# Turning the first quad's maxima into PSUM bank 5 instead of bank 7

## The chip, the cores and the metric

The kernel runs on one core of a Trainium2 chip. A time is the device time of one launch in microseconds (us). A comparison is made between medians of several launches on the same chip.

## What is computed

Two layers of a small transformer, on x of shape 2 x 512 x 128 and a context of 2 x 154 x 128, all in float32 with reference accuracy:

```python
x = x + L0_xattn(layernorm(x), ctx, ctx, Wq, bq, Wk, bk, Wv, bv, Wo, bo)   # 16 heads of 8
x = x + L0_ffn(layernorm(x), ...)      # 8 experts, each takes its top 128 tokens
x = x + L1_xattn(layernorm(x), ctx, mask, W_attn)                          # one head, masked
x = x + L1_ffn(layernorm(x), ...)      # 32 experts of width 64, top 8 per token, and a shared one
```

The change lies in the first of the four, the attention of 16 heads:

```python
scores = einsum('bhqd,bhkd->bhqk', q, k) / sqrt(HEAD_DIM)
attn = softmax(scores, axis=-1)
out = einsum('bhqk,bhkd->bhqd', attn, v) @ Wo.T + bo
```

## The kernel before

The kernel is one program per engine, written out by hand. TensorE (`pe`), VectorE (`dve`), ScalarE (`act`), GpSimd (`pool`) and SyncE (`sp`, DMA issues) each run their list of steps in the order in which it is written, and every dependence is a wait on a semaphore that another engine counts up. An engine that waits holds up all that stands behind the wait in its list.

PSUM is one tensor `bank` of 8 banks with 512 float32 columns each. The first attention works in quads: 4 heads of one batch of 512 queries, 8 quads in all, called `cc` 0 to 7. For a quad, the steps are:

- `keys(g)` multiplies the keys of head group g (4 groups, both batches) into `keys_bank(g)`: bank 3, 4, 7 and 7. ScalarE copies them with their bias to `kh`, rounded to a shorter format; VectorE's `k_lo(g)` (L540) reads the bank again and writes the rounding error beside it, partitions 64 to 95. The semaphore `klo_ready` counts these. `expand` (GpSimd L388, for quad 0 VectorE L598) spreads the keys of a group over a block per head in `ks`.
- `turned`, `first_queries` and `all_queries` make the queries. For quads 1 to 7 three DMA copies each (`laid`, L337, L338, L340) bring them to their partitions in `qs`; semaphores `laid0` and `laid1`.
- `rough(cc, part)` (L1383) makes trial products of queries and keys. VectorE's `maxima(cc, part)` (L572) reduces them to the largest value for each query and head, into `smax`; semaphore `max_done`. For quad 0 there are two parts, which lie in banks 0 to 2 and 3 to 5; for the others six, in banks 0 to 2.
- TensorE's `maxima(cc)` turns `smax` by four transposes (helper `turn`, L1302) into bank 7, and ScalarE's `minus_max(cc)` (L1008) copies the result, negated, into `qs` as extra rows, so that `scores` (L1428) gives scores minus the maximum. Semaphores `mT_psum` and `mT_ready`.
- `scores`, ScalarE's `exponents` (L1054) and `attend` (L1442, into bank 5, first at `attend(0, 0)`) are the softmax and the products with the values; `values` (L1376) makes the values in bank 6.

Two helpers on TensorE guard the banks that many steps share. `take7` waits for the reader of whoever used bank 7 before, and notes who will be the next reader:

```python
free7 = [(Z["klo_ready"], 4)]

def take7(sem_, count):
    pe.wait_ge(*free7[0])
    free7[0] = (sem_, count)
```

The first user of bank 7 after the last group's keys is `maxima(0)`, so that it waits for `klo_ready` at 4, that is `k_lo(3)`. Bank 5 is first used for the gate sums (L1516); ScalarE reads them out (L1046, semaphore `gsum_ready`), and the second part of quad 0's trial products, which reaches into bank 5, waits for that.

Around the change the orders are, on TensorE: `rough(0, 0)`, `all_queries(0)`, `keys(3)`, `rough(0, 1)`, four filling products (`early_work`, L1328, bank 0), `maxima(0)`, `values(0, 0)`, `scores(0, 0)`, `rough(1, 0)`. On VectorE:

```python
maxima(0, 0)
all_q_lo(0)
maxima(0, 1)
k_lo(3)
dve.wait_ge(L["x1"], 16)
second = measure(x, TB)
maxima(1, 0)
```

`measure` takes the statistics of the second half of x (L504 to L514); GpSimd raises the variance to the power -0.5 (L368) and VectorE centres that half (L526) after `maxima(1, 3)`. On SyncE the load of `fc1` (2048 KB, L344) stands between the copies for quad 3 and those for quad 4.

Of the kernel before, what the change touches and what calls it, by code (L numbers as in the profile page):

```python
# [13 lines left out]
P = 128  # L14
# [3 lines left out]
TB = T // B  # L18
# [10 lines left out]
HQ = HH // 2  # L29
QW = HQ * DH  # L30
KQ = 3 * QW + HQ
QUADS = 2 * COMBOS
QSLOTS = 6
# [51 lines left out]
def maxes(cc, part):  # L85

    return part + 1 if cc == 0 else 2 + PARTS * (cc - 1) + part + 1
# [13 lines left out]
def build(nc, x_d, ctx2_d, mask_d, watt_d, pack_d, rows_d, gate_d, fc1_d, fc2_d, wout_d, wr_d, rec_d,  # L101
          bd_d, out_d):
    with ExitStack() as ctx:
        def sb(name, shape, dt=F32):
            return ctx.enter_context(nc.sbuf_tensor(name, shape, dt))

        def sem(name):
            return ctx.enter_context(nc.semaphore(name))

        def lay(base, names, parts=P):  # L110

            out, at = [], 0
            for shape in names:
                n = int(np.prod(shape[1:]))
                v = base[0:shape[0], at:at + n]
                ax = "abcd"[:len(shape) - 1]
                if len(shape) > 2:
                    v = v.rearrange(f"p ({' '.join(ax)}) -> p {' '.join(ax)}",
                                    **{a: m for a, m in zip(ax, shape[1:])})
                out.append(v)  # L120
                at += n
            assert at <= base.shape[1], (at, base.shape)
            return out

        bank = ctx.enter_context(nc.psum_tensor("bank", [P, 8, 512], F32))
# [29 lines left out]
        qs, ks = lay(arena_a, ([P, QSLOTS, S], [P, QUADS, HBLK * P]))  # L155
# [46 lines left out]
        smax = sb("smax", [P, 2 * TB, QW + HQ])  # L202
# [67 lines left out]
        Z = {n: sem(n) for n in names}  # L270
# [695 lines left out]
        def _(act):  # L966
# [37 lines left out]
            def minus_max(cc):  # L1004

                r0, turns = (0, cc) if cc < 2 else (cc % 2 * QW, 1 + cc // 2)
                act.wait_ge(Z["mT_psum"], turns + 1)
                act.mul(qs[3 * QW:KQ, cc % QSLOTS, :], bank[r0:r0 + HQ, 7, :], -1.0).then_inc(Z["mT_ready"], 1)  # L1008

            def with_bias(b, c0=0, c1=S):  # L1010
                act.wait_ge(Z["at_psum"], b + 1 + (c0 > 0))
# [47 lines left out]
            act.wait_ge(L["late"], 48)  # L1059
            indicators(act.copy, 0)  # L1060
            minus_max(0)
            exponents(0, 0)
            exponents(0, 1)
# [4 lines left out]
            turned(1)  # L1068
            exponents(0, 4)
            minus_max(1)  # L1070
            all_queries(1)
            exponents(0, 5)
            exponents(0, 6)
            exponents(0, 7)
            exponents(0, 8)
            exponents(0, 9)
            minus_max(2)
            minus_max(3)
            exponents(1, 0)
# [220 lines left out]
        def _(pe):  # L1300
            def turn(dst, src, n=P):
                return pe.transpose(dst, src, ident[0:n, 0:n])  # L1302
# [17 lines left out]
# [4 lines that stand above are left out]
# [83 lines left out]

            def maxima(cc, both=False):

                take7(Z["mT_ready"], cc + 1 + both)  # L1410
                pe.wait_ge(Z["max_done"], maxes(cc + both, PARTS - 1 if cc else 1))
                q0, q1 = (0, QW + HQ) if both else (cc % 2 * QW, cc % 2 * QW + HQ)
                for i in range(TB):
                    ins = turn(bank[0:q1 - q0, 7, i * P:(i + 1) * P], smax[:, cc // 2 % 2 * TB + i, q0:q1])
                ins.then_inc(Z["mT_psum"], 1)

            def scores(c, i):
# [105 lines left out]
            pe.wait_ge(Z["max_done"], 1)  # L1523
            early_work(4, 0)
            maxima(0)
            values(0, 0)
            scores(0, 0)
# [12 lines left out]
            turned(1)  # L1540
            rough(2, 1)
            maxima(1)
            all_queries(1)
            rough(2, 2)
# [16 lines left out]
            attend(0, 1)  # L1561
            rough(4, 1)
            maxima(2, both=True)
            rough(4, 2)
            rough(4, 3)
# [89 lines left out]
            for b in range(B):  # L1655
                pe.matmul(bank[0:SH, 0, b * D:(b + 1) * D], ctx2[:, b, 0:SH], wout[:, 0, :], start=True, stop=True)
                ins = pe.matmul(bank[0:SH, 0, (B + b) * D:(B + b + 1) * D], ctx2[:, b, SH:SK], wout[:, 0, :],
                                start=True, stop=True)
# [49 lines left out]
            for t in range(T):  # L1708
                ins = pe.matmul(upto, onesb[:, :], gteq[:, 0, t, None, :].broadcast_to([P, T, E0]),
                                start=False, stop=(t == T - 1))  # L1710
# [422 lines left out]
```

## Time and profile before

| | us |
|---|---|
| median of 3 runs | 244.21 (244.19 to 244.49) |
| the profiled execution | 244.43 |
| its span | 242.6 |

| engine | busy us | share of the span |
|---|---|---|
| TensorE, products | 224.3 | 92% |
| TensorE, weight loads | 157.4 | 65% |
| VectorE | 175.9 | 72% |
| ScalarE | 128.8 | 53% |
| GpSimd | 74.6 | 31% |

The profile is of one execution. Times within it are counted from the start of its span. In the rows PE is TensorE and PEld its weight loads, DVE is VectorE, ACT is ScalarE, POOL is GpSimd, SPq is SyncE's DMA queue. A float32 product appears as two MATMUL instructions. L1302 is the line of the helper `turn`, so all transposes carry it; their operands tell them apart, and `smax` means the turns of maxima. An idle time in brackets is that of the engine before the first instruction of the row, with what ended it. The chain is followed back from the last instruction; "issue" in it is time in which an engine waited for nothing visible.

### The profile page before, as it was taken

What the parts mean: (1) busy time and instruction counts of PE and PEld (TensorE: products, weight loads), DVE (VectorE), ACT (ScalarE), POOL (GpSimd) and SP (SyncE); (2) the same over time, 40 slices, a digit from 0 to 9 for tenths busy, and PEclk for the clock granted to TensorE, in tenths of its full rate; (3) what the DMA queues carried; (4) which work ended last, traced back from release to release, by engine and by line L of the source; (5) the groups of instructions that cost most, each with busy time, mean ns of one, the idle gap of its engine ahead of it and who ended that gap; (6) DMA issues with size and microseconds to landing.
All of it is one profiled execution on the core that took longest, in us unless ns stands there. A gap on an engine that the chain in (4) does not pass through costs nothing.

```text
span 242.6 us, 3703 instructions
## 1 busy us (share of the span) xinstructions
PE 224.3 (92%) x1220; PEld 157.4 (65%) x1228; DVE 175.9 (72%) x436; ACT 128.8 (53%) x262; POOL 74.6 (31%) x113
## 2 busy tenths in 40 slices
PE   8979998999997888999999998889999999999993
PEld 2446544655564344678687966667888888888871
DVE  2689766663376887796351787999888879888883
ACT  2427557678536921442544766666454555554551
POOL 6235997020430600000490303000453353353000
PEclk9999999999999999999999999979999999999999
DMA  6316739300000000000052000000112212200002
GB/s 226 123 43 195 263 87 352 118 0 0 3 0 0 1 0 4 0 0 3 1 139 80 0 3 1 0 0 0 46 43 49 81 47 48 83 0 0 3 0 86
DMA packets 6152, 12.92 MB, mean 53 GB/s; under 512 B 1139, under 2 KB 2259, under 8 KB 5878
## 3 DMA queue, kind: packets, MB, share of 16 engines
q1 hardware_dynamic: 5302, 11.91, 15.8%
q10 hardware_dynamic: 832, 0.78, 1.0%
q8 instruction: 10, 0.16, 0.3%
q14 instruction: 8, 0.07, 0.1%
HBM read 10.78 MB, written 0.52 MB: 47 GB/s over the span
## 4 chain that ended last, share of the span: by engine, by line
PE 74%; DVE 18%; ACT 3%; issue 3%; POOL 1%; DVEq 0%; another core or an unknown queue 0%; ACTq 0%; POOLq 0%
PE bank L1939 6%; PE bank L1943 6%; PE bank L1940 6%; PE bank L1302 5%; PE bank L1442 5%; PE bank L1428 5%; DVE att L707 4%; PE bank L1383 4%; PE bank L1973 3%; PE bank L1789 3%; PE bank L1976 3%; PE bank L1328 3%; PE bank L1974 3%; PE bank L1954 3%; PE bank L1776 3%
## 5 line engine op out<-in xcount | busy, mean ns | idle before, releaser
L1242 ACT ACTIVATE arena_d<-bank,bias 128x512 f32<-128x512 f32 x34 | 23.4, 689 | 32.3 <-PE bank L1943 32.3
L893 DVE SCALAR_TENSOR_TENSOR arena_d<-bank,bias,arena_d 128x512 f32<-128x512 f32 x34 | 25.5, 750 | 9.5 <-ACT arena_d L1242 9.2
L572 DVE TENSOR_REDUCE smax<-bank 128x3 f32<-128x462 f32 (+2 forms) x44 | 25.2, 619 | 8.4 <-PE bank L1383 8.3
L1054 ACT ACTIVATE arena_c<-bank 128x512 f32<-128x512 f32 x40 | 22.6, 598 | 10.2 <-PE bank L1442 5.4
L471 POOL CAST arena_b<-rec 128x512 fp32r<-128x512 f32 x17 | 13.4, 788 | 46.7 <-PE bank L1976 46.6
L1939 PE MATMUL bank<-arena_b 128*128 128x512 f32 x68 | 27.1, 399 | 0.1
L1943 PE MATMUL bank<-arena_b 128*128 128x512 f32 x68 | 27.1, 398 | 0.0
L1940 PE MATMUL bank<-arena_b 128*128 128x512 f32 x68 | 27.0, 397 | 0.0
L907 DVE TENSOR_TENSOR arena_a<-arena_d,arena_a 128x512 fp32r<-128x512 f32 x34 | 23.5, 691 | 0.8 <-ACT arena_a L1249 0.7
L1249 ACT CAST arena_a<-arena_d 128x512 fp32r<-128x512 f32 x34 | 20.8, 612 | 3.2 <-DVE arena_d L902 2.9
L902 DVE TENSOR_TENSOR arena_d<-arena_d,bank 128x512 f32<-128x512 f32 x32 | 21.8, 681 | 0.4 <-PE bank L1954 0.3
L368 POOL TENSOR_TENSOR rstd<-vareps,neghalf 128x4 f32<-128x4 f32 x8 | 8.1, 1012 | 38.5 <-DVE vareps L514 28.5
L1383 PE MATMUL bank<-arena_a 96*128 96x462 f32 (+3 forms) x64 | 17.6, 353 | 0.6 <-DVE smax L572 0.4
L1308 PE MATMUL bank<-pack,onesb 128*128 128x512 bf16 x66 | 17.3, 378 | 0.3
L1428 PE MATMUL bank<-arena_a 100*128 100x512 f32 x40 | 17.3, 454 | 0.0
L474 POOL TENSOR_TENSOR arena_b<-rec,arena_b 128x384 fp32r<-128x384 f32 x17 | 16.3, 961 | 1.4
L1383 PEld LDWEIGHTS bank<-arena_a 96*128 96x128 f32 x64 | 11.3, 189 | 7.6 <-DVE smax L572 3.1
L1943 PEld LDWEIGHTS bank<-arena_b 128*128 128x128 f32 x68 | 13.1, 192 | 3.2 <-DVE arena_b L858 0.4
L1939 PEld LDWEIGHTS bank<-arena_b 128*128 128x128 f32 x68 | 12.9, 190 | 3.2 <-issue 0.3
L1940 PEld LDWEIGHTS bank<-arena_b 128*128 128x128 f32 x68 | 13.0, 191 | 2.7
L1973 PE MATMUL bank<-arena_a,arena_b 128*128 128x512 f32 x34 | 13.9, 408 | 0.3 <-ACT arena_a L1249 0.3
L1976 PE MATMUL bank<-arena_a,arena_b 128*128 128x512 f32 x34 | 13.6, 399 | 0.1
(256 smaller groups left out, 477.1 us busy)
## 6 DMA issues: line engine op xcount, KB each, us to landing
rec<-in_rec SPq DMA_DIRECT2D x17, 257.0 KB, 2.6
arena_d<-in_fc SPq DMA_DIRECT2D x1, 2048.0 KB, 9.2
fc<-in_fc SPq DMA_DIRECT2D x1, 2048.0 KB, 7.8
arena_a<-yhi SPq DMA_DIRECT2D x14, 64.0 KB, 2.0
x<-in_x SPq DMA_DIRECT2D x2, 256.0 KB, 4.2
out<-x SPq DMA_DIRECT2D x2, 256.0 KB, 2.0
arena_a<-ylo SPq DMA_DIRECT2D x7, 64.0 KB, 2.0
pack<-in_pack ACTq DMA_DIRECT2D x1, 382.0 KB, 5.6
```

The lines of the kernel that those rows point to most:

```text
L572: dve.tensor_reduce(dst, src, AX.X, ALU.max).then_inc(Z["max_done"], 1)
L893: dve.scalar_tensor_tensor(to[:, k % 2, :], bank[:, 2 + k % 2, :], bias[:, u % SPLITS, 1:2], sil[:, k % 2, :], ALU.add, ALU.mult).then_inc ...
L902: dve.tensor_tensor(hh[:, k % 2, :], gu[:, k % 2, :], bank[:, 5 - k % 2, :], ALU.mult)\
L907: dve.tensor_tensor(hlo[:, k % 2, :], hh[:, k % 2, :], f32(hhi[:, k % 2, :]), ALU.subtract)\
L1054: act.activation(pT[:, n % RING, :], bank[:, 3 + n % 2, :], ACT.Exp, scale=float(DH) ** -0.5)\
L1242: act.activation(sil[:, k % 2, :], bank[:, k % 2, :], f, bias=bias[:, STEPS[k][0] % SPLITS, 0:1])\
L1383: return pe.matmul(to, qs[0:3 * QW, cc % QSLOTS, t * P:(t + 1) * P], ks[0:3 * QW, cc, k0:k1], start=True, stop=True)
L1428: pe.matmul(bank[:, 3 + n % 2, :], ks[0:KQ, cc, j * P:(j + 1) * P], qs[0:KQ, cc % QSLOTS, :], start=True, stop=True).then_inc(Z["score_psu ...
L1939: pe.matmul(d, whi[:, r, w], y3hi[:, cs], start=True, stop=False)
L1940: pe.matmul(d, wlo[:, r, w], y3hi[:, cs], start=False, stop=False)
L1943: ins = pe.matmul(d, whi[:, r, w], y3lo[:, cs], start=False, stop=True)
L1973: pe.matmul(d, whi[:, r, w], hhi[:, k % 2, :], start=(k == ONSET[b]), stop=False, skip_group_check=True)
```

## The change

The turns of quad 0's maxima write bank 5, and ScalarE reads them there. TensorE's `maxima(0)` no longer calls `take7`; it waits for `gsum_ready` instead. The other quads stay in bank 7.

```diff
--- before.py
+++ after.py
@@ -1005,7 +1005,7 @@
 
                 r0, turns = (0, cc) if cc < 2 else (cc % 2 * QW, 1 + cc // 2)
                 act.wait_ge(Z["mT_psum"], turns + 1)
-                act.mul(qs[3 * QW:KQ, cc % QSLOTS, :], bank[r0:r0 + HQ, 7, :], -1.0).then_inc(Z["mT_ready"], 1)
+                act.mul(qs[3 * QW:KQ, cc % QSLOTS, :], bank[r0:r0 + HQ, 7 if cc else 5, :], -1.0).then_inc(Z["mT_ready"], 1)
 
             def with_bias(b, c0=0, c1=S):
                 act.wait_ge(Z["at_psum"], b + 1 + (c0 > 0))
@@ -1407,11 +1407,14 @@
 
             def maxima(cc, both=False):
 
-                take7(Z["mT_ready"], cc + 1 + both)
+                if cc:
+                    take7(Z["mT_ready"], cc + 1 + both)
+                else:
+                    pe.wait_ge(Z["gsum_ready"], 1)
                 pe.wait_ge(Z["max_done"], maxes(cc + both, PARTS - 1 if cc else 1))
                 q0, q1 = (0, QW + HQ) if both else (cc % 2 * QW, cc % 2 * QW + HQ)
                 for i in range(TB):
-                    ins = turn(bank[0:q1 - q0, 7, i * P:(i + 1) * P], smax[:, cc // 2 % 2 * TB + i, q0:q1])
+                    ins = turn(bank[0:q1 - q0, 7 if cc else 5, i * P:(i + 1) * P], smax[:, cc // 2 % 2 * TB + i, q0:q1])
                 ins.then_inc(Z["mT_psum"], 1)
 
             def scores(c, i):
```

No instruction is added, dropped or moved. What differs on TensorE are the waits of two steps. First the turns of quad 0, before and after the change (4x128 rows; the brackets name the semaphores that a row waits for):

```order
L1328 MATMUL bank<-onesb 128x512 [waits max_done]
L1328 MATMUL bank<-onesb 128x512 x3
L1302 MATMUL bank<-pack,smax 4x128 [waits max_done,klo_ready]
L1302 MATMUL bank<-pack,smax 4x128 x3
L1376 MATMUL bank<-watt,ctx 128x128 [waits alllo_ready,ld_late]
L1376 MATMUL bank<-watt,ctx 128x128 x3
L1428 MATMUL bank<-arena_a 128x512 [waits k_first,qlo_ready,mT_ready]
L1383 MATMUL bank<-arena_a 128x462 [waits max_done,expanded,laid1]
```

```order
L1328 MATMUL bank<-onesb 128x512 [waits max_done]
L1328 MATMUL bank<-onesb 128x512 x3
L1302 MATMUL bank<-pack,smax 4x128 [waits max_done,gsum_ready]
L1302 MATMUL bank<-pack,smax 4x128 x3
L1376 MATMUL bank<-watt,ctx 128x128 [waits alllo_ready,ld_late]
L1376 MATMUL bank<-watt,ctx 128x128 x3
L1431 MATMUL bank<-arena_a 128x512 [waits k_first,qlo_ready,mT_ready]
L1383 MATMUL bank<-arena_a 128x462 [waits max_done,expanded,laid1]
```

The first turn waits for `gsum_ready` in place of `klo_ready`; the line numbers behind it differ since three lines were added. Then the turns of quad 1, before and after:

```order
L1428 MATMUL bank<-arena_a 128x512 [waits exp_done]
L1302 MATMUL bank<-pack,xn 128x128 [waits xn_ready,vraw_ready]
L1302 MATMUL bank<-pack,xn 128x128 x3
L1383 MATMUL bank<-arena_a 128x462 [waits max_done]
L1302 MATMUL bank<-pack,smax 4x128 [waits max_done,mT_ready]
L1302 MATMUL bank<-pack,smax 4x128 x3
```

```order
L1431 MATMUL bank<-arena_a 128x512 [waits exp_done]
L1302 MATMUL bank<-pack,xn 128x128 [waits xn_ready,vraw_ready]
L1302 MATMUL bank<-pack,xn 128x128 x3
L1383 MATMUL bank<-arena_a 128x462 [waits max_done]
L1302 MATMUL bank<-pack,smax 4x128 [waits max_done,klo_ready]
L1302 MATMUL bank<-pack,smax 4x128 x3
```

As `maxima(1)` is now the first to take bank 7 after the keys, the wait for `klo_ready` stands there, in place of that for `mT_ready`.

## Rows read from the trace of the kernel before

**Rows 1.** The page: span, granted clock, chain by engine.

```profile
span 242.6 us, 3703 instructions
...
PEclk9999999999999999999999999979999999999999
...
PE 74%; DVE 18%; ACT 3%; issue 3%; POOL 1%; DVEq 0%; another core or an unknown queue 0%; ACTq 0%; POOLq 0%
```

**Rows 2.** The chain that ended last, 14 to 24 us (start us, us, what).

```profile
15.39 1.35 DVE smax L572
...
16.77 0.55 DVE arena_e L540
...
17.36 0.60 PE bank L1302 x4
...
21.50 1.04 DVE xn L526 x4
```

**Rows 3.** Timeline: start us, us, engine, line, ... xcount, [idle before <-releaser].

```profile
15.30 1.43 DVE L572 TENSOR_REDUCE smax<-bank 128x8 f32<-128x1232 f32 x1
15.87 0.59 SPq L340 DMA_DIRECT2D arena_a<-ylo  x1
...
16.77 0.54 DVE L540 SCALAR_TENSOR_TENSOR arena_e<-bank,pack,arena_e 32x308 fp32r<-32x308 f32 x1
...
17.36 0.31 PEld L1302 LDWEIGHTS bank<-pack,smax 128*4 128x4 f32 x4 [1.95 <-DVE arena_e L540]
17.36 0.60 PE L1302 MATMUL bank<-pack,smax 128*4 128x128 f32 x4 [1.46 <-DVE arena_e L540]
...
17.99 0.59 ACT L1008 ACTIVATE arena_a<-bank 4x512 fp32r<-4x512 f32 x1 [2.58 <-PE bank L1302]
...
18.73 0.16 DVE L514 TENSOR_SCALAR vareps<-mv 128x4 f32<-128x4 f32 x1
18.74 0.42 PEld L1383 LDWEIGHTS bank<-arena_a 96*128 96x128 f32 x2
...
18.98 1.02 POOL L368 TENSOR_TENSOR rstd<-vareps,neghalf 128x4 f32<-128x4 f32 x1 [0.38 <-DVE vareps L514]
```

**Rows 4.** Timelines again: quad 1's reductions and turns, quad 4's copy and load.

```profile
19.38 2.12 DVE L572 TENSOR_REDUCE smax<-bank 128x3 f32<-128x462 f32 x4 [0.48 <-PE bank L1383]
...
22.99 0.47 DVE L572 TENSOR_REDUCE smax<-bank 128x2 f32<-128x308 f32 x1
...
23.57 0.08 PEld L1302 LDWEIGHTS bank<-pack,smax 128*4 128x4 f32 x1 [0.26 <-issue]
...
27.15 0.59 SPq L340 DMA_DIRECT2D arena_a<-ylo  x1
...
30.91 0.19 PEld L1383 LDWEIGHTS bank<-arena_a 96*128 96x128 f32 x1 [0.55 <-issue]
```

**Rows 5.** Copy issued at 15.87, fc1, copy of 27.15: last column, us to landing.

```profile
arena_a<-ylo SPq DMA_DIRECT2D x1, 64.0 KB, 2.0
...
arena_d<-in_fc SPq DMA_DIRECT2D x1, 2048.0 KB, 9.2
...
arena_a<-ylo SPq DMA_DIRECT2D x1, 64.0 KB, 3.0
```

**Rows 6.** TensorE by stretch (length, busy, clock, DMA), then two pieces of chain.

```profile
16.70:17.40 0.70, 0.04 (x1) 1.00 0.40 100
...
157.20:160.60 3.40, 3.40 (x9) 0.50 0.00 0
160.60:164.00 3.40, 2.41 (x11) 1.00 0.00 0
164.00:167.40 3.40, 3.09 (x15) 1.00 0.00 0
...
159.84 0.44 issue
...
165.86 0.23 PE bank L1939
```

## The prediction

> **What bounds the kernel now.** I read the page first. The chain that ended last is 74% TensorE and 18% VectorE, and TensorE's granted clock is full in every slice but one [rows 1]. So the span follows TensorE with a few handovers, and an edit at one handover is read from the chain there. The chain between 14 and 24 us [rows 2] shows the place of the change: VectorE reduces the second half of quad 0's products (L572, 15.39 to 16.74), then corrects the last group's keys (L540, 0.55 us), and only then do the four turns of quad 0's maxima start, at 17.36. The third view is the timeline [rows 3]. It names L540 as what released the load of the turns, not the reduction, and gives both sides: the reduction ends at 15.30 + 1.43 = 16.73, L540 runs from 16.77 to 17.31, and the first weight load of the turns is at 17.36. In between TensorE does nothing and its queue is held in order: the turns, the value products (L1376), the first scores (L1428) and quad 1's first trial product (L1383, load at 18.74) all stand behind that wait. VectorE stands still once more ahead of 19.38, 0.48 us, for that trial product [rows 4].
>
> **What the change does to each instruction.** Nothing is added, dropped or moved: TensorE's rows stand in the same order with the same shapes, and so do those of the other engines. Three things differ.
>
> (1) The turns of quad 0 write bank 5 and no longer wait for the last group's keys. Their other wait, for the second reduction, stays. When would the load start? The nearest case is the same pair one quad later: a reduction starts at 22.99 and takes 0.47, and the turns' load comes at 23.57, that is 0.11 us after its end [rows 4]. Here that gives 16.73 + 0.11 = 16.84, and 17.36 - 16.84 = 0.52 us is saved at the turns. The other bound is the delay seen behind L540 itself, 17.36 - 17.31 = 0.05 [rows 3], which gives 16.78 and 0.58 us. I take 0.52, as that pair has the same two instructions and the same two waits.
>
> (2) The wait that takes the place of the old one is for the copy of the gate sums out of bank 5. The trial products of quad 0's second half have that wait already, and the reduction behind which the turns start reads just these products; so it is met before it is asked, and costs nothing. Bank 5 is next written by the first attend products; they stand in TensorE's queue behind the scores of quad 0, and these wait for the negated maxima. So no new wait arises there.
>
> (3) The wait for the keys is not gone but handed on: the second call of the turns, for quad 1, now makes it. Its load is at 23.57 [rows 4], while the keys are done at 17.31: met 6.3 us earlier, cost nothing. The old wait of that call, for ScalarE's read of quad 0's maxima in bank 7, has lost its object. ScalarE's read of bank 5 instead of 7 is the same 4x512 instruction, 0.59 us.
>
> **What is late next.** Behind the turns everything on TensorE moves with them: the value products need bank 6, whose last reader stands ahead of the reduction in VectorE's list. ScalarE's negation follows the last turn, at 17.99; it has been idle 2.58 us [rows 3], so it moves by the same amount and keeps its place ahead of the scores. The trial product's load goes from 18.74 to 18.22. It needs quad 1's three copies: the last is issued at 15.87 and lands 2.0 us later [rows 3, 5], at 17.87, so 0.35 us is to spare. This is the first point where the gain could have ended, and it doesn't.
>
> The second point is VectorE. Its reduction of quad 1 at 19.38 would be released at 18.86. But VectorE's own work does not move: L540, then the statistics of the second half of x, whose last instruction ends at 18.73 + 0.16 = 18.89 [rows 3]. Of the 0.52 us therefore 19.38 - 18.89 = 0.49 arrives (an instruction may start before the one ahead of it has ended: the reduction starts at 15.30 in the timeline [rows 3], while the chain has it only from 15.39 [rows 2], 0.09 later; so all 0.52 may). I take 0.50. Even an ideal start of the turns at 16.73 could bring no more than 19.38 - 18.80 = 0.58 here: from this place VectorE is the bound, four reductions of 2.12 us in one piece.
>
> Third, the centring of x (L526, 21.50 in the chain [rows 2], 21.00 after the change) needs GpSimd's power, which ends at 18.98 + 1.02 = 20.00 and does not move [rows 3]. Spare: 1.0 us. GpSimd's expansion of the last group's keys waits for L540 as before; its reader is quad 3's trial product, which stands in TensorE's list behind the turns of quad 1 at 23.57. No loss.
>
> Fourth, quad 4's copies. Their issue follows the second half's queries, which follow TensorE, so they move too; but a weight load of 2048 KB, issued behind quad 3's copies and 9.2 us under way [rows 5], does not move, and the copies share the DMA engines with it. The last of the three is issued at 27.15 [rows 4] and takes 3.0 us in place of 2.0, landing at 30.15. Its reader loads at 30.91 [rows 4], after the change at 30.41. Even a landing that did not move at all would be 0.26 us early. Cost 0, and it is a rival below.
>
> After that every start in the trace hangs on TensorE or on an engine that follows it, up to the end: the gain neither grows nor is used up. **Sum:** -0.50 us, bounds -0.58 above and -0.44 below: the latter if the 0.05 us of a release (17.31 to 17.36) comes on top of VectorE's 18.89, which makes 0.49 - 0.05.
>
> **The clock.** TensorE's 1.46 us of rest before the turns shrinks to about 0.9. Its clock is granted in full right through the rest (1.00 from 16.7 to 17.4) and before and after it [rows 1, 6], so a shorter rest gives back nothing. The Trainium skill (TensorE: Matmul & The Clock Gate, Part 1) has the clock halved after too little work on TensorE, by a monitor that runs freely, so that a kernel meets it at another phase in each execution. By the row the sum stays -0.50; by the rule it stays so as well, but single executions differ.
>
> **From this to the time.** The profiled execution took 244.43 us, 1.83 more than its span of 242.6. It would become 243.93. The median of the three runs is 244.21, the lower two are 244.19 and 244.21. The profiled one has a stretch at half clock (1.2 GHz in place of 2.4), 157.2 to 160.6 [rows 6], in which the chain shows 0.44 us of waiting for nothing visible at 159.84. TensorE gets through 8 products there, 3.40 / 8 = 0.43 us each, in place of the 0.23 that one takes in the chain at 165.86. I take it, as an estimate from the spread of the times, that this is worth the 0.2 to 0.3 between 244.2 and 244.43 or 244.49. The forecast is for the median: 244.21 - 0.50 = 243.71 us.
>
> **Rivals.**
> (a) *The clock falls otherwise.* If the median run of the changed kernel has such a stretch and the one of before had none, 0.25 to 0.3 of the gain is hidden: 243.95 to 244.0. For it: the three times fall into two groups. Against it: two of three are in the low one. 12%. By the Trainium skill's free-running monitor the chance is the same for either kernel, so this rival has its mirror image in (d).
> (b) *The copies or the statistics take part of it.* If the larger load holds quad 4's last copy until 30.65 rather than 30.15, its reader starts 0.24 late and the gain is 0.26: 243.95. It decides from a landing at 30.41. Or VectorE's reduction needs longer between the statistics and its start than the rows show. 10%.
> (c) *The change doesn't do what it says:* another wait, not L540, held the turns. Against it: 0.05 us between L540's end and the load, and the reduction had ended 0.63 us before the load. 244.2. 3%.
> (d) *More than the sum:* full 0.58 at the turns and at VectorE, or the low-clock stretch absent in the median: 243.4 to 243.6. 7%.
> (e) *Slower.* TensorE rests again before 164.0 (2.41 us busy of 3.40 from 160.6 on), and right behind that the chain is TensorE's own, at 0.23 us a product [rows 6]. Everything arrives there 0.5 us earlier; if the half clock then covered 164 to 167.4 instead of the stretch in which VectorE leads, 8 products would cost 0.20 us more each, 1.6 us: 244.21 - 0.50 + 1.6 = 245.3. It decides from an extra cost of 1.0 us. Against it: after this very rest the trace of before shows the full clock, 1.00 from 164.0 to 167.4. 4%.
>
> **Chances.** The forecast itself has 64%. The bound of 0.2%, about what a measurement of this kernel can tell from no change, is 0.49 us, a time of 243.72, and lies in the middle of it: of the 64% I give 39 to faster and 25 to within. With (d) faster is 46%; with (a), (b) and (c) the same is 50%; slower 4%. The range runs from 243.45, the 0.58 us and a run-to-run tenth and more, to 244.10, past (a) and (b).
>
> **What would show it.** In the profile of the changed kernel the turns' load at 16.8 names the reduction L572 as its releaser, or nothing, and TensorE's idle before it falls from 1.46 to about 0.9; L540 stays put; VectorE's idle before quad 1's first reduction falls from 0.48 to 0; centring moves by 0.5, and quad 4's reader is near 30.4; the span is 242.1 if the half-clock stretch is there again. The forecast is wrong if the turns start at 16.8 and a later row, say the read at 30.91, has not moved: then something fixed lies between, and its place is where the two traces rejoin.

## The result and the profile after

| | us |
|---|---|
| median after | 243.69 (243.30 to 244.15, 19 runs) |
| median before, same chips | 243.94 (243.74 to 244.54, 19 runs) |
| ratio | 0.9984, interval 0.9977 to 0.9992 |
| profiled execution, span | 243.80, 242.0 (before 244.43, 242.6) |

The ratio stands for 0.39 us, with an interval from 0.20 to 0.56: a small gain, inside 0.2% by its middle. The plain medians lie only 0.25 us apart; such a difference between two ways of comparing the same executions is the size of their scatter. A second measurement gave 0.9985 (0.9977 to 0.9994).

The page of the changed kernel (span, granted clock by slice, chain by engine):

```profile
span 242.0 us, 3703 instructions
...
PEclk9999999999999999999999999979999999999999
...
PE 72%; DVE 19%; ACT 3%; issue 3%; DMA 2%; POOL 1%; SPq 0%; DVEq 0%; another core or an unknown queue 0%; ACTq 0%; POOLq 0%
```

Its chain from 14 to 24 us; [rows 2] has the same stretch of before:

```profile
15.18 1.35 DVE smax L572
...
16.56 0.54 DVE arena_e L540
...
17.12 0.88 DVE stats L504 x4
...
18.03 0.39 DVE mv L511 x4
...
18.44 0.17 DVE negmean L513
18.61 0.07 DVE vareps L514
...
18.72 2.12 DVE smax L572 x4
20.83 1.03 DVE xn L526 x4
...
22.00 0.63 PE bank L1302 x4
```

The chain no longer leaves VectorE for the turns. Behind the keys (L540) it stays on VectorE, through the statistics (L504, L511, L513, L514), straight into the reductions of quad 1 at 18.72. The turns have become work beside it.

Its timeline at the same instructions [rows 3, 4], and the load of quad 4's first trial product:

```profile
15.09 1.43 DVE L572 TENSOR_REDUCE smax<-bank 128x8 f32<-128x1232 f32 x1
...
16.56 0.54 DVE L540 SCALAR_TENSOR_TENSOR arena_e<-bank,pack,arena_e 32x308 fp32r<-32x308 f32 x1
16.64 0.33 PEld L1302 LDWEIGHTS bank<-pack,smax 128*4 128x4 f32 x4 [1.45 <-issue]
16.67 0.60 PE L1302 MATMUL bank<-pack,smax 128*4 128x128 f32 x4 [0.98 <-DVE smax L572]
...
17.30 0.58 ACT L1008 ACTIVATE arena_a<-bank 4x512 fp32r<-4x512 f32 x1 [2.11 <-PE bank L1302]
...
18.52 0.16 DVE L514 TENSOR_SCALAR vareps<-mv 128x4 f32<-128x4 f32 x1
...
18.72 1.18 DVE L572 TENSOR_REDUCE smax<-bank 128x3 f32<-128x462 f32 x2
...
30.25 0.19 PEld L1383 LDWEIGHTS bank<-arena_a 96*128 96x128 f32 x1 [0.55 <-DMA arena_a<-ylo]
```

The reduction ends at 15.09 + 1.43 = 16.52 and the turns' load is at 16.64, 0.12 later, while L540 is still running. TensorE's rest is 0.98 in place of 1.46. VectorE goes from L514 into the reduction without a rest. This execution began 0.21 us earlier than that of before (L540 at 16.56 against 16.77), so each shift is read from L540 on:

| from L540's start to | before | after | gain |
|---|---|---|---|
| the turns' load | 0.59 | 0.08 | 0.51 |
| quad 1's first reduction | 2.61 | 2.16 | 0.45 |
| quad 4's first load | 14.14 | 13.69 | 0.45 |

So 0.51 us is won at the turns, 0.45 passes VectorE, and all of that is still there 12 us on. Spans differ by 0.62: the 0.21 of the start and 0.41, that is 0.45 less a few hundredths.

### The profile page after: what moved, and what is told of

Read it like the earlier page. It is cut to its first block, busy times and chain, and to the rows that moved or that the text cites. A ratio compares the mean times of both kernels' runs of the same rounds, so it can differ in the third digit from the quotient of the medians.

```text
span 242.0 us, 3703 instructions
## 1 busy us (share of the span) xinstructions
PE 224.2 (93%) x1220; PEld 157.3 (65%) x1228; DVE 175.8 (73%) x436; ACT 128.7 (53%) x262; POOL 74.5 (31%) x113
## 4 chain that ended last, share of the span: by engine, by line
PE 72%; DVE 19%; ACT 3%; issue 3%; DMA 2%; POOL 1%; SPq 0%; DVEq 0%; another core or an unknown queue 0%; ACTq 0%; POOLq 0%
PE bank L1942 6%; PE bank L1946 6%; PE bank L1943 6%; PE bank L1302 5%; PE bank L1445 5%; DVE att L707 4%; PE bank L1431 4%; PE bank L1976 3%; PE bank L1792 3%; PE bank L1979 3%; PE bank L1977 3%; PE bank L1328 3%; PE bank L1383 3%; PE bank L1957 3%; PE bank L1779 3%
## 5 line engine op out<-in xcount | busy, mean ns | idle before, releaser
L572 DVE TENSOR_REDUCE smax<-bank 128x3 f32<-128x462 f32 (+2 forms) x44 | 25.2, 617 | 8.0 <-PE bank L1383 7.9
L902 DVE TENSOR_TENSOR arena_d<-arena_d,bank 128x512 f32<-128x512 f32 x32 | 21.8, 680 | 0.4 <-PE bank L1957 0.2
```

Source lines behind the costliest of these rows:

```text
L572: dve.tensor_reduce(dst, src, AX.X, ALU.max).then_inc(Z["max_done"], 1)
L902: dve.tensor_tensor(hh[:, k % 2, :], gu[:, k % 2, :], bank[:, 5 - k % 2, :], ALU.mult)\
```

## The experiments

Twelve further runs were made, two of them repeats (after_again and after_late_again); the ratios are against the kernel of before, measured beside each. For the reading of the traces one table serves all that bear on the change. Each column is a difference of starting times in one trace: from L540 to the turns' load, to quad 1's first reduction (L572), and to the first counting instruction of the expert choice (L707, 75.50 us in the trace of before), far behind the attention.

| kernel | ratio (interval) | turns | reduction | L707 |
|---|---|---|---|---|
| before | 1 | 0.59 | 2.61 | 58.73 |
| bank_only | 1.0007 (0.9998 to 1.0016) | 0.59 | 2.61 | 58.78 |
| before_extra | 1.0012 (1.0003 to 1.0021) | 0.60 | 2.62 | 58.79 |
| before_early | 1.0005 (0.9992 to 1.0018) | 0.59 | 2.61 | 58.76 |
| before_late | 1.0002 (0.9993 to 1.0012) | 0.59 | 2.62 | 58.76 |
| changed | 0.9984 (0.9977 to 0.9992) | 0.08 | 2.16 | 58.32 |
| after_again | 0.9985 (0.9977 to 0.9994) | 0.08 | 2.16 | 58.29 |
| after_extra | 0.9993 (0.9984 to 1.0002) | 0.09 | 2.50 | 58.63 |
| after_early | 0.9987 (0.9976 to 0.9999) | 0.08 | 2.12 | 58.26 |
| after_late | 0.9977 (0.9968 to 0.9986) | 0.08 | 2.16 | 58.30 |
| after_late_again | 0.9977 (0.9969 to 0.9986) | 0.08 | 2.16 | 58.32 |

Where nothing is changed, the first two distances repeat to 0.01 us and the third to 0.04 in the changed kernel and 0.06 in that of before; the ratios scatter more (up to 0.0012, or 0.3 us, between kernels with the same distances). The traces carry the argument. The three runs with fewer fillers, at the end, have the same distances: 0.59, 2.61 and 58.76 with the old wait, 0.08, 2.16 and 58.31 to 58.33 without it.

### Is it the wait, or the bank?

The changed kernel with the old wait put back, still into bank 5:

```diff
                 else:
+                    pe.wait_ge(Z["klo_ready"], 4)
                     pe.wait_ge(Z["gsum_ready"], 1)
```

> The changed kernel, but its first turns wait for the last group's keys again, still into bank 5. My theory (the gain is the 0.5 us of that wait): the turns' load stands 0.05 us behind L540 again, VectorE rests about 0.48 us before quad 1's first reduction, and the time is that of before, within 0.1 us. Rival (the bank itself matters, one that no other engine reads at that time): the time stays 0.3 to 0.5 us below before.

Its timeline, where L540, the turns' load and quad 1's first reduction stand:

```profile
16.52 0.54 DVE L540 SCALAR_TENSOR_TENSOR arena_e<-bank,pack,arena_e 32x308 fp32r<-32x308 f32 x1
...
17.11 0.31 PEld L1302 LDWEIGHTS bank<-pack,smax 128*4 128x4 f32 x4 [1.95 <-DVE arena_e L540]
...
19.13 1.18 DVE L572 TENSOR_REDUCE smax<-bank 128x3 f32<-128x462 f32 x2 [0.48 <-PE bank L1383]
```

Load 0.05 us behind L540's end, 0.48 us of rest before the reduction, median 244.02 against 243.90. It is the kernel of before in every distance. Bank 5 by itself is worth nothing that the trace or the ratio (1.0007) shows; the gain is the wait's.

And the changed kernel again:

> The changed kernel once more, as the anchor of this call: 0.3 to 0.5 us below before by my theory. Up to the first keys it is the same kernel, so its trace should differ from that of before by a constant there, which comes from the input DMAs, and by a further 0.46 us from quad 1's first reduction on.

```profile
16.11 0.54 DVE L540 SCALAR_TENSOR_TENSOR arena_e<-bank,pack,arena_e 32x308 fp32r<-32x308 f32 x1
16.19 0.33 PEld L1302 LDWEIGHTS bank<-pack,smax 128*4 128x4 f32 x4 [1.45 <-issue]
...
18.27 2.12 DVE L572 TENSOR_REDUCE smax<-bank 128x3 f32<-128x462 f32 x4
```

Median 243.57. The same 0.08 and 2.16 as in the first trace of the changed kernel, though this execution stands 0.45 us further ahead at L540. The extra shift at the reduction is 0.45, as expected to 0.01. That the input DMAs alone make the constant in front of it did not hold: the last experiments show where it comes from.

### Is VectorE the bound behind the change?

One idle instruction of VectorE, behind the last group's keys, in either kernel:

```diff
             k_lo(3)
             dve.wait_ge(L["x1"], 16)
+            dve.tensor_scalar(res_spare[:, :], x[:, TB:, :].rearrange("p t d -> p (t d)"), 1.0, None, ALU.mult)
             second = measure(x, TB)
```

> The kernel of before with one idle VectorE instruction (a copy of 128x512 values that nobody reads) behind the last group's keys, of length d, some 0.3 to 0.6 us. My theory: VectorE has 0.48 us to spare there, so the time grows by d - 0.48 at most, that is by nothing up to 0.15 us. Rival (VectorE's list is not what decides at that place in either kernel): no change either. The pair with after_extra tells them apart.

> The changed kernel with the same idle VectorE instruction. My theory: VectorE is the bound behind the change, so all of d (0.3 to 0.6 us) is lost: quad 1's first reduction comes d later, and with d of 0.5 or more the kernel is as slow as before with the same instruction. Rival (TensorE's release decides, VectorE has slack): no change, the kernel stays 0.4 us below before.

Before with it, then the changed kernel with it (lines of the file stand one or two further down; L541 is L540, L573 is L572):

```profile
16.68 0.54 DVE L541 SCALAR_TENSOR_TENSOR arena_e<-bank,pack,arena_e 32x308 fp32r<-32x308 f32 x1
...
17.25 0.43 DVE L634 TENSOR_SCALAR res_spare<-x 128x512 f32<-128x512 f32 x1
17.28 0.31 PEld L1304 LDWEIGHTS bank<-pack,smax 128*4 128x4 f32 x4 [1.95 <-DVE arena_e L541]
...
19.30 1.18 DVE L573 TENSOR_REDUCE smax<-bank 128x3 f32<-128x462 f32 x2
```

```profile
16.18 0.54 DVE L541 SCALAR_TENSOR_TENSOR arena_e<-bank,pack,arena_e 32x308 fp32r<-32x308 f32 x1
16.27 0.33 PEld L1304 LDWEIGHTS bank<-pack,smax 128*4 128x4 f32 x4 [1.45 <-issue]
...
16.75 0.43 DVE L634 TENSOR_SCALAR res_spare<-x 128x512 f32<-128x512 f32 x1
...
18.49 0.16 DVE L515 TENSOR_SCALAR vareps<-mv 128x4 f32<-128x4 f32 x1
...
18.68 1.57 DVE L573 TENSOR_REDUCE smax<-bank 128x3 f32<-128x462 f32 x3
```

The instruction takes 0.43 and, as instructions overlap, holds what follows up by 0.34. In the kernel of before the reduction stays where it was (2.62 against 2.61): its slack of 0.48 swallows it. In the changed kernel the reduction comes 0.34 later (2.50 against 2.16), and 0.31 to 0.34 of it arrive at L707 (58.63 against 58.29 to 58.32). So VectorE has 0.48 us to spare before the change and none after it. The rival, that TensorE's release decides, is out. The ratio of before_extra (1.0012, its interval just above 1) doesn't follow its distances: 4 of its 11 executions took 244.41 to 244.53 at a mean clock of 0.992 or 0.993, the group of which the last experiments tell, and none of the 33 of before measured beside it did.

The other way round, the four statistics instructions moved ahead of the first keys, where VectorE rests:

```diff
             norm(x, xn, 0, "xn_ready")
+            dve.wait_ge(L["x1"], 16)
+            norms[0] += 1
+            for i in range(TB):
+                ins = dve.bn_stats(stats[:, 1, i, :], x[:, TB + i, :])
...
             k_lo(3)
-            dve.wait_ge(L["x1"], 16)
-            second = measure(x, TB)
+            dve.wait_ge(Z["dve_chain"], chain[0])
+            second = aggregate(norms[0])
```

> The kernel of before, with the four statistics instructions on the second half of x (0.87 us of VectorE) moved ahead of the first keys, where VectorE rests 1.2 us. My theory: VectorE was not the bound behind L540, so nothing comes of it: no change, within 0.1 us.

> The changed kernel with the same move. My theory: VectorE is free 0.87 us sooner, so that TensorE's release decides about quad 1's first reduction: the shift there goes from 0.46 to 0.51 us, and the time falls by 0.05 us beside the changed kernel, which only the trace can tell. Rival (VectorE's list holds much more than the trace shows): 0.2 us or more.

Before with it, then the changed kernel with it (L546 is L540, L578 is L572):

```profile
16.35 0.53 DVE L546 SCALAR_TENSOR_TENSOR arena_e<-bank,pack,arena_e 32x308 fp32r<-32x308 f32 x1
...
16.94 0.31 PEld L1308 LDWEIGHTS bank<-pack,smax 128*4 128x4 f32 x4 [1.95 <-DVE arena_e L546]
...
18.96 1.19 DVE L578 TENSOR_REDUCE smax<-bank 128x3 f32<-128x462 f32 x2 [0.68 <-PE bank L1389]
```

```profile
16.32 0.53 DVE L546 SCALAR_TENSOR_TENSOR arena_e<-bank,pack,arena_e 32x308 fp32r<-32x308 f32 x1
16.40 0.33 PEld L1308 LDWEIGHTS bank<-pack,smax 128*4 128x4 f32 x4 [1.45 <-issue]
...
16.93 1.22 POOL L388 TENSOR_TENSOR arena_a<-arena_e,pack 100x616 fp32r<-100x616 f32 x1 [3.46 <-DVE arena_e L546]
...
17.30 0.87 DVE L513 TENSOR_SCALAR negmean<-mv 128x4 f32<-128x4 f32 x1
...
18.08 0.16 DVE L514 TENSOR_SCALAR vareps<-mv 128x4 f32<-128x4 f32 x1
...
18.44 2.12 DVE L578 TENSOR_REDUCE smax<-bank 128x3 f32<-128x462 f32 x4 [0.20 <-PE bank L1389]
```

Before: no change (2.61), VectorE just rests longer, 0.68. Changed: VectorE rests 0.20 and TensorE's release decides; the reduction stands at 2.12, 0.04 us further ahead, where the forecast had 0.05. That is all there is behind VectorE: TensorE comes right after it, and 0.49 of the 0.51 us at the turns then gets through. The medians (244.06 and 243.66) can't show 0.04 us.

### Do the copies of quad 4 take part of it?

In the changed kernel's trace the last of these copies, issued at 26.48, takes longer than in [rows 5], by its row of DMA issues (last column, us to landing):

```profile
arena_a<-ylo SPq DMA_DIRECT2D x1, 64.0 KB, 3.7
```

It lands at 26.48 + 3.7 = 30.18; before it was 27.15 + 3.0 = 30.15. The landing has not moved, while the reader has moved to 30.25. The trace names the copy as the last thing it waited for, and the chain that ended last runs through it, which it did not before. So I moved the large load behind all copies:

```diff
-            sp.dma_start(fc1[:, :, :], fc1_d).then_inc(L["fc1"], 16)
             for cc in range(4, QUADS):
                 laid(cc)
+            sp.dma_start(fc1[:, :, :], fc1_d).then_inc(L["fc1"], 16)
```

> The kernel of before with the 2048 KB load of fc1 issued behind all the copies of queries instead of ahead of those of quad 4. My theory: quad 4's last copy lands 1 us sooner after its issue, but its reader had 0.7 us to spare already; no change, within 0.1 us. Rival (the copies of quads 4 to 7 hold TensorE somewhere in the 28 to 40 us stretch): faster by 0.1 us or more.

> The changed kernel with the same later load. In the trace of the changed kernel quad 4's last copy landed at 30.2, no earlier than before, and its reader loaded at 30.25, so the spare time is used up. My theory: in that profiled run it costs nothing yet, so at most 0.1 us is to be had here. Rival (the shared DMA engines take part of the gain in many executions): faster than the changed kernel by 0.1 to 0.2 us, that is 0.5 us or more below before.

> The changed kernel with the later fc1 load, a second time, since its first median (243.49, 0.9977 of before) was the lowest. My theory: at the full clock it is the changed kernel, so its ratio to before is that of the changed kernel, 0.998 to 0.9985, and the trace shows no gain from it; rival (the copies take part of the gain): 0.9977 or below again.

The reader in the trace of after_late:

```profile
29.91 0.19 PEld L1383 LDWEIGHTS bank<-arena_a 96*128 96x128 f32 x1 [0.55 <-issue]
```

Its distance from quad 1's first reduction is 29.91 - 18.37 = 11.54; it is 11.53 both before and in the changed kernel, and 11.51 in after_again, where the trace names the copy too (29.78 - 18.27). With the large load out of the way the copies take 2.0 us again, and nothing is gained in the trace: the landing at 30.18 cost nothing, though it came only 0.07 us ahead of the reader. The kernel before_late gives 1.0002, as expected. But both measurements of after_late read 0.9977 (medians 243.49 and 243.44), against 0.9984 and 0.9985. By the ratio that is what the rival said in both expectations, and the second measurement missed the 0.998 to 0.9985 that my theory gave. The intervals overlap, and among executions at the full clock the two kernels have the same median, 243.43 (the table below). So it is not shown that the copies take something in other executions; no trace shows where it would be. It is a rival that the runs leave open, at 0.1 to 0.2 us; as the later load costs nothing, this is the version that I would keep, 0.9977 of before.

### What parts the executions?

Leaving out the measurement with fewer fillers, the times of the others for which clocks are on record fall into groups by the mean clock of each execution (four at 0.987 are left out):

| mean granted clock | before | changed | changed, fc1 late |
|---|---|---|---|
| above 0.993 | 243.91 (72 runs) | 243.43 (13) | 243.43 (16) |
| 0.992 or 0.993 | 244.47 (12) | 243.71 (15) | 243.58 (6) |

In the upper row the change is worth 0.48 us, close to the 0.41 to 0.45 of the traces; in the lower row the medians lie 0.76 apart, more than the change can be worth by any trace. The lower row holds 12 of 84 executions of before and 15 of 28 of the changed kernel. A median over both rows therefore hides part of the gain. Why the changed kernel fell into the lower row more often, no run shows.

I had put 0.2 to 0.3 us of this down to the half-clock stretch at 157 us. A trace of the changed kernel has such a stretch and one has none. The first, by stretches of TensorE (length, busy, granted clock, DMA):

```profile
156.80:160.20 3.40, 3.40 (x10) 0.50 0.00 0
160.20:163.60 3.40, 2.19 (x10) 1.00 0.00 0
```

The other, after_again, has none; the first rows are its start, the last three its chain at the place of [rows 6]:

```profile
1.17 4.79 PE L1328 MATMUL bank<-onesb 128*128 128x512 bf16 x14 [1.17 <-POOL onesb L375]
5.80 1.20 PE L1338 MATMUL bank<-ctx,watt 128*96 128x308 f32 x4
...
158.75 0.09 issue
...
158.86 0.35 issue
159.21 0.68 DVE arena_d L902
```

The chain has 0.09 + 0.35 = 0.44 us of "issue" before L902 at the full clock too. So the 0.44 that I read in [rows 6] is not the clock's: VectorE leads there. The rest of the program settles it. From L707 to the end of the span it is 167.12 us in the trace of before and 167.12 in that of the changed kernel, both with a stretch, and 167.10 to 167.17 in the ten traces without one. Of the four with a stretch only before_extra takes longer, 167.21: there the chain runs through TensorE's products at that place, 0.43 us each. So the stretch at 1.2 GHz cost nothing in three traces and up to 0.1 us in one. The start is what differs. In the trace of before:

```profile
1.17 6.08 PE L1328 MATMUL bank<-onesb 128*128 128x512 bf16 x14 [1.17 <-POOL onesb L375]
7.08 1.20 PE L1338 MATMUL bank<-ctx,watt 128*96 128x308 f32 x4
```

The 14 fillers take 6.08 us there, 0.43 us for each 512 columns, which is 1.2 GHz nearly to the end, and the first keys stand behind them at 7.08. (The view of the granted clock prints 1.00 from 1 to 7 us, so that only the pace tells: it is that of the products in the stretch at 157 us, where the view reads 0.50.) In after_again they take 4.79 and the keys start at 5.80. L540 follows at 16.77 and 16.11. An execution whose clock rises late starts up to 0.66 us late. The Trainium skill (TensorE: Matmul & The Clock Gate, Part 1) says that the phase in which an execution meets the clock's monitor is free and varies from run to run; the traces agree (keys at 5.80, 6.07 and 6.88 in three executions whose first part is the same program).

The late start and the stretch at 157 us are not one thing. The trace of bank_only has the late start and no stretch, and its 244.22 us at a mean clock of 0.999 stands among the executions at the full clock:

```profile
1.17 5.84 PE L1328 MATMUL bank<-onesb 128*128 128x512 bf16 x14 [1.17 <-POOL onesb L375]
6.84 1.20 PE L1338 MATMUL bank<-ctx,watt 128*96 128x308 f32 x4
```

So I took fillers away:

```diff
             pe.wait_ge(Z["consts_ready"], 3)
-            early_work(14, 7)
+            early_work(11, 7)
```

> The kernel of before with 11 filling products ahead of the first keys in place of 14 (fillers are computed and read by nobody). In the trace of before the 14 take 6.08 us at half clock and the first keys start behind them at 7.08; in a trace whose clock rose sooner they take 4.79 and the keys start at 5.80, and everything later stands 0.66 us earlier. My theory: the executions in which the clock rises late are slow because of the fillers, and that, not the half-clock stretch at 157 us, parts the times of before (243.9 and 244.5). With 11 fillers the slow executions fall to 244.0 or below, the fast ones stay at 243.9. Rival (the stretch at 157 us costs the 0.5 us): the executions with a stretch still take 244.4 or more.

> The changed kernel with the later fc1 load and 11 fillers. My theory: 243.4 in all executions, 0.5 us below before, with a narrower spread than 243.36 to 243.61. If fewer fillers let the clock rise later, the queries and first trial products run at half clock and it is slower by 0.3 us or more.

> The same with 9 fillers, which end near 5 us even at half clock, before the keys' operands have landed. By my theory of the start nothing more is gained than with 11, 243.4; TensorE rests between fillers and turns, so that the clock may rise later, which would cost 0.3 us or more and show as half clock beyond 7 us.

The trace of before_fill11:

```profile
1.17 4.78 PE L1328 MATMUL bank<-onesb 128*128 128x512 bf16 x11 [1.17 <-POOL onesb L375]
5.78 1.20 PE L1338 MATMUL bank<-ctx,watt 128*96 128x308 f32 x4
7.86 0.63 PE L1302 MATMUL bank<-pack,xn 128*128 128x128 f32 x4 [0.87 <-DVE xn L526]
```

The keys start at 5.78, but the turns of xn behind them (the transposes of the centred first half of x) wait until 7.86, for VectorE: the first half of x came late in this execution. The medians are 244.19 against 244.33 (0.9996, 0.9987 to 1.0005), 243.68 (0.9979, 0.9969 to 0.9990) and 243.71 (0.9984, 0.9969 to 0.9998). Of the executions of before_fill11 with a clock of 0.993 one took 243.89 and one 244.63, and others without a stretch took up to 244.58. My expectations failed: before_fill11 still has executions above 244.2, and with 11 and 9 fillers the changed kernel took up to 244.30 and 245.28 where 243.4 was forecast for all. The executions of before measured beside them were spread evenly from 243.84 to 244.64 too.

For the executions that have a trace, the rows part the two sources of this scatter. The columns are starting times: of VectorE's first statistics, which wait for the first half of x; of the first keys; of the turns of xn; of the last group's L540.

| trace | fillers | x's statistics | keys | turns of xn | L540 | stretch at 157 us |
|---|---|---|---|---|---|---|
| before | 14 | 3.42 | 7.08 | 8.12 | 16.77 | yes |
| changed | 14 | 3.52 | 6.88 | 7.92 | 16.56 | yes |
| bank_only | 14 | 3.49 | 6.84 | 7.88 | 16.52 | no |
| after_late | 14 | 3.52 | 6.07 | 7.54 | 16.21 | no |
| after_again | 14 | 3.41 | 5.80 | 7.43 | 16.11 | no |
| before_fill11 | 11 | 3.83 | 5.78 | 7.86 | 16.53 | no |
| after_late_fill11 | 11 | 3.55 | 5.50 | 7.57 | 16.25 | no |
| after_late_fill9 | 9 | 3.78 | 5.29 | 7.80 | 16.48 | yes |

In the first three the turns of xn follow the keys by 1.04 us and L540 stands 9.68 or 9.69 us behind the keys: the fillers at half clock decide. In the other five the turns wait for VectorE's xn, and L540 stands 12.69 or 12.70 us behind the statistics: the landing of x decides. So fewer fillers can take away only the first kind of lateness, and a late x is left, 0.42 us between the earliest and the latest here. Whether a late x makes the slow executions that have no trace is not shown.

## Why the prediction was right, and where not

- **The place and the mechanism.** The turns waited for L540 and nothing else. Shown by bank_only.
- **0.52 us at the turns** [rows 4]: 0.51 in the trace, with a load 0.12 us behind the reduction where 0.11 was taken from quad 1's pair. The bound of 0.58 was not reached.
- **VectorE as the next bound.** Right, and shown from both sides by the extra instruction and the early statistics. The size was a little off: I took 0.50 between 0.49 and 0.52 because instructions can overlap. They didn't here. The reduction starts 0.04 us after L514 ends (18.52 + 0.16, 18.72), which is my lower bound of 0.44 plus a hundredth. An overlap seen between two instructions whose operands were ready was no reason to expect one before the first reduction of a new quad.
- **What costs nothing.** The wait for the gate sums and the handed-on wait for the keys (quad 1's turns at 22.90 in the changed kernel, keys done at 17.10) cost nothing. The centring kept its spare time.
- **The copies** were costed at nothing, since even a landing that did not move would be 0.26 us early. It did not move, and 0.07 was left: the execution had started 0.2 us earlier, which moved the reader and left the landing where it was. The sum stands, but a spare time read from one trace should have been set beside the scatter of the start.
- **The clock.** This is the step that failed. I read 0.44 us of "issue" in the half-clock stretch as its price and explained the groups of times by it. The same 0.44 stands in a trace without a stretch, and from L707 to the end the traces with and without one take the same time. In the traces the times part at the start, and I had taken the clock there as full from the page [rows 1], though the fillers ran at 0.43 us each. Rival (a) then half came true by another way than I gave: the changed kernel has more of its executions in the lower row of the table.
- **The level.** 243.71 was forecast and 243.69 measured, but from 244.21 less 0.50; the larger sample has before at 243.94, and the gain was 0.39 by the ratio and 0.25 by the medians. The nearness of the two numbers is luck; the gain is the thing to compare, 0.50 forecast and 0.41 to 0.48 by traces and by the executions at the full clock. It lies at the 0.2% mark, where I had put the chances for faster and the same nearly even.

## What to carry to other kernels

When a wait is taken away, find the engine that released it and read how much work of its own still stands before the next handover: here it capped 0.51 at 0.45, and the cap could be read from four rows. Count shifts from a common instruction near the change, since two executions may start 0.66 us apart with the same program up to there. And before a gap in the chain is put down to a slow clock, look for the same gap in an execution at full clock.

## What the hardware showed that I had not expected

With the statistics moved away, VectorE's 128x4 instruction L513 starts at 17.30 and takes 0.87 us in place of 0.17, in the rows of after_early above. It runs until GpSimd's L388 ends (16.93 + 1.22 = 18.15). In before_early the same instruction takes 0.88. The statistics (L504) beside the same GpSimd instruction were not held up: 0.88 for four in the chain of the changed kernel above. The Trainium skill (SBUF — State Buffer, Who interferes with whom) has VectorE and GpSimd share a port pair by an exclusive lock, which VectorE's two-port forms need. Duration and end agree with that; that L513 ran in such a form is not recorded. So of the 0.87 us of work moved away 0.70 was lost again in this wait; the measured 0.04 is not smaller for it, since TensorE's release decided there in any case.
